# A two-layer attention and expert kernel: first tokens and first queries prepared one stage early, choices spread two pairs ahead, 64-row masks

## The reference

```python
xn = layernorm(x)
s = attention0(xn)            # 16 heads of 8, scores_content + scores_pos, softmax, @ Wo + bo
g = silu(expert_of_argmax(xn))  # 8 experts, one chosen per token, D x D each, with bias
x = x + s * g
xn = layernorm(x)
s = attention1(xn)            # 8 heads of two 8-wide halves, causal:
                              #   softmax(half 0) - lam * softmax(half 1), then rms norm, @ Wo
g = silu(top-2 of 8 experts)  # each 128 -> 256 -> 128 with gelu
x = x + s * g
```

## Time and profile before

| | us |
|---|---|
| median of 3 runs | 2071.6 (2067.59 to 2082.31) |
| profiled execution, its own time | 2077.91 |
| its span, first to last instruction | 2076.1 |
| token stage 0 | 0 to 213 |
| attention stage 0 | about 216 to 1203 |
| token stage 1 | about 1205 to 1519 |
| attention stage 1 | about 1522 to 2076 |
| PE busy over the span | 1767.2 (85%) |
| DVE, ACT, POOL busy | 1325.2 (64%), 1195.4 (58%), 1146.4 (55%) |

### The profile page before, as it was taken

One profiled execution on the slowest core, in us unless ns is written; L12 is line 12 of the kernel. 1 busy time (PEld: TensorE's weight loads), 2 busy tenths in 40 slices (PEclk: granted clock), 3 DMA queues, 4 the chain that ended last, 5 costly groups with the idle time before them and its releaser, 6 DMA issues. The chain is left out here.

```text
span 2076.1 us, 78586 instructions
## 1 busy us (share of the span) xinstructions
PE 1767.2 (85%) x34080; PEld 1327.7 (64%) x34080; DVE 1325.2 (64%) x1965; ACT 1195.4 (58%) x1438; POOL 1146.4 (55%) x1502
## 2 busy tenths in 40 slices
PE   5887489998898998989999759999968978879886
PEld 4666377777777776778877536666735545546554
DVE  5442367777676766877777424445467868867883
ACT  2322167777677766777877623344416645656555
POOL 4742469997699858998898621221112333333433
PEclk9887699999999999999999869999979989979998
DMA  3456312123221241222121121133220131121110
GB/s 104 129 146 191 93 52 66 48 65 96 73 65 59 67 106 60 68 68 59 55 62 55 52 91 53 57 95 88 80 61 18 30 66 26 41 52 30 26 26 16
DMA packets 166300, 139.97 MB, mean 67 GB/s; under 512 B 91715, under 2 KB 157014, under 8 KB 160454
## 3 DMA queue, kind: packets, MB, share of 16 engines
q1 hardware_dynamic: 153370, 105.93, 17.9%
q10 hardware_dynamic: 7212, 16.42, 3.3%
q0 software_dynamic: 5376, 12.59, 2.2%
HBM read 90.98 MB, written 43.12 MB: 65 GB/s over the span
## 5 line engine op out<-in xcount | busy, mean ns | idle before, releaser
L1306 ACT ACTIVATE a_EX<-bank 128x1024 f32<-128x1024 f32 x624 | 616.1, 1025 | 292.4 <-PE bank L1178 227.4
L1425 DVE TENSOR_TENSOR a_PM<-bank,a_PM 128x1024 f32<-128x1024 f32 x336 | 402.2, 1222 | 169.0 <-PE bank L1178 156.8
L1265 POOL TENSOR_TENSOR a_SN<-a_SN,a_MB 128x1024 f32<-128x1024 f32 x176 | 421.1, 2429 | 46.3 <-DMA a_MB<-m_dram 45.1
L1448 DVE TENSOR_REDUCE a_M<-bank 128x2 f32<-128x1024 f32 (+3 forms) x304 | 340.3, 1165 | 85.5 <-PE bank L1191 54.9
L1388 PE MATMUL bank<-a_EX,VV 128*32 128x128 f32 x9984 | 360.0, 288 | 3.5 <-issue 1.8
L1178 PE MATMUL bank<-QS,KS 51*128 51x128 bf16 (+1 forms) x4992 | 237.9, 230 | 89.5 <-DMA QS<-a_MP 38.1
L1388 PEld LDWEIGHTS bank<-a_EX,VV 128*32 128x32 f32 x9984 | 270.8, 115 | 52.1 <-issue 22.9
L1178 PEld LDWEIGHTS bank<-QS,KS 51*128 51x128 bf16 (+1 forms) x4992 | 160.1, 100 | 183.1 <-issue 57.6
L1302 ACT ACTIVATE a_SN<-bank 128x1024 f32<-128x1024 f32 x176 | 177.2, 1026 | 93.6 <-PE bank L1158 92.5
L1310 ACT ACTIVATE a_SN<-a_SN 128x1024 f32<-128x1024 f32 x176 | 185.4, 1058 | 38.8 <-POOL a_SN L1265 38.5
L1158 PE MATMUL bank<-QP,rel_t 112*128 112x32 bf16 x5632 | 197.7, 177 | 1.4 <-issue 1.2
(11 more groups left out here) (151 smaller groups left out, 2487.8 us busy)
## 6 DMA issues: line engine op xcount, KB each, us to landing
a_MB<-m_dram SPq DMA_DIRECT2D x32, 1024.0 KB, 4.9
QS<-q_dram SPq DMA_DIRECT2D x192, 96.0 KB, 3.0
KS<-k_dram ACTq DMA_DIRECT2D x12, 768.0 KB
q_dram<-t_PARTS SPq DMA_DIRECT2D x32, 192.0 KB, 2.8
k_dram<-t_PARTS SPq DMA_DIRECT2D x16, 384.0 KB, 2.9
QS<-a_MP SPq DMA_DIRECT2D x384, 2.0 KB
q_dram<-t_PARTS SPq DMA_DIRECT2D x32, 128.0 KB, 2.6
k_dram<-t_PARTS SPq DMA_DIRECT2D x16, 256.0 KB, 2.9
```

Source lines behind the costliest of these rows:

```text
L1265: pool.tensor_tensor(near_view(sn), near_view(sn), as_near(MB[:, :, :], it.part), ALU.add)\
L1306: act.activation(as_banks(EX[:, it.need % ER[layer]], part), by_head, ACT.Exp, scale=SCALE).then_inc(act_done, 1)
L1425: dve.tensor_tensor(pm, mb.rearrange("p hh (k i) -> p hh k i", k=4), pm, ALU.max).then_inc(max_used, 1)
L1448: dve.tensor_reduce(target.rearrange("p (hh k) -> p hh k", hh=2)[:, :, p0:p0 + g], mb[:, :, 0:g * width].rearrange("p hh (k j) -> p hh k j ...
```

## The change

- POOL permutes the queries of units 0 and 1 of layer 0 at the end of token stage 0 (after `parts` of the last group) instead of at the start of the attention stage; `permute` is now a helper.
- The first group of layer 1 (loading X, statistics, reciprocal root, normalisation) moves into attention stage 0: POOL loads X1 at `final` of unit 28, DVE takes the statistics after `final` of unit 30, POOL computes the root before its `final` of unit 31, DVE normalises before its `final` of unit 31. SP loads the q, k and v projections of layer 1 at `final` of unit 28. Their buffers lie in the half of KR that layer 0's batch 2 has left.
- SP no longer ends a token stage with the wait for `g_stored`; POOL waits for the group of the unit in `load_xg`, and ACT for all groups before it writes OS for unit 0 (OS and G now share memory). The exponentials for lam move to ACT's start of attention stage 0, after the key loads, and the rest to DVE's `final` of unit 0.
- The choice of pair 0 is spread at front 6, that of pair 1 at front 7, and at expert step k the choice of pair k+4 after the wait for HM of pair k.
- A mask tile is 4 matmuls of 256 columns: for each half of the queries (or keys) a weight table of 64 x 128 selects, and a moving table of 64 x 64, repeated for four heads, carries the values; the output has a step of two floats.
- For layer 1 the planner's mask cost goes from 480 to 260, and AIM, NEAR_BY and STAY are new. Layer 0's plan is the same.

```diff
-        "mask": 480, "evict": 1028, ...
+        "mask": 260, "evict": 1028, ...
-    {"max": (-0.94, 0.96), "mrow": (-5.54, -2.26), "msplit": (-1.51, -3.76), "exp": (1.3, 0.81),
-     "av": (4.27, -0.7), "out": (2.15, 1.46)}]
-NEAR_BY, STAY = (179, 222), (0.55, 1.3)
+    {"max": (-0.89, 0.93), "mrow": (-5, -1.11), "msplit": (-2.16, -1.22), "exp": (1.31, 0.71),
+     "av": (4.53, -0.91), "out": (2.07, 1.41)}]
+NEAR_BY, STAY = (179, 493), (0.55, 0.47)
...
+        OS = sb("OS", [P, 512])
+        G = OS[:, :].rearrange("p (t d) -> p t d", d=P)
+        spare = KR[:, 0, :, :].rearrange("p a s -> p (a s)").bitcast(F32)
+        X1 = spare[:, 0:512].rearrange("p (t d) -> p t d", d=P)
+        XN1 = spare[:, 512:1536].rearrange("p (c t d) -> p c t d", c=2, d=P)
...
+        def permute(pool, u):
+            r, q = u % NR, u % QR
+            pool.wait_ge(q_in[0][q], 64 * (u // QR + 1))
+            for a in range(2):
+                ... (the two copies and the drain, as before)
...  token stage, POOL
-                    scale(0)
-                    load_x(1)
-                    scale(1)
+                    if layer == 0:
+                        scale(pool, layer, 0)
+                    fetch_x(1)
+                    scale(pool, layer, 1)
...
                     parts(GROUPS - 1)
+                    if layer == 0:
+                        for u in range(NR):
+                            permute(pool, u)
...  token stage, SP
-                    sp.wait_ge(g_stored, 16 * GROUPS + 1)
...  token stage, ACT and DVE: the lam steps are taken out
-                        act.wait_ge(lam_sum, 1)
-                        act.activation(lam_s[:, 0:2], lam_s[:, 0:2], ACT.Exp).then_inc(lam_exp, 1)
...  token stage, PE
                             if k % 2 == 0:
-                                if k + 2 < E:
-                                    spread_choice(f, k + 2)
                                 pe.wait_ge(xm_ready, f * (E // 2) + k // 2 + 1)
+                                if k + 4 < E:
+                                    spread_choice(f, k + 4)
...
-                        if kind == "front" and k == 7 and layer == 0:
-                            spread_choice(f, 0)
+                        if kind == "front" and k >= 6 and layer == 0:
+                            spread_choice(f, 2 * (k - 6))
...  attention stage
-                for part in range(2):
+                for half in range(2):
                     for hh in range(2):
                         rows = slice(hh * HALF, (hh + 1) * HALF)
-                        last = pe.matmul(bank[:, 2 * it.n + hh, :].rearrange("p (h c) -> p h c", h=4), mask_b[rows, 0, part, :],
-                                         mask_b[rows, which, part, None, :].broadcast_to([HALF, 4, P]), start=False,
-                                         stop=part == 1, skip_group_check=True)
+                        out_h = bank[:, 2 * it.n + hh, :].rearrange("p (h c a) -> p h c a", h=4, a=2)[:, :, :, half]
+                        last = pe.matmul(out_h, mask_b[rows, which, half * P:(half + 1) * P],
+                                         mask_b[rows, which, None, 2 * P:].broadcast_to([HALF, 4, HALF]), start=False, stop=True,
+                                         skip_group_check=True)
...  SP, at final of a unit in layer 0
+                                if u == UNITS - 4:
+                                    sp.wait_ge(av_done, spare_free)
+                                    load_projections(sp, 1)
...  POOL
                     def load_xg(u):
+                        pool.wait_ge(g_stores[layer], 16 * (row_of(u) // GT + 1) + 1)
...
+                        if it.kind == "perm" and u >= NR:
+                            pool.wait_ge(act_psum, it.need + 1)
+                            permute(pool, u)
...
                         elif it.kind == "final":
+                            if layer == 0 and u == UNITS - 1:
+                                scale(pool, 1, 0)
...
+                            if layer == 0 and u == UNITS - 4:
+                                pool.wait_ge(av_done, spare_free)
+                                for r in range(2):
+                                    pool.wait_ge(stored[r], 16 * GT // 2)
+                                load_x(pool, 1, dst, X1, 0)
...  ACT
                     load_kv(layer, act, 1)
+                    if layer == 0:
+                        act.wait_ge(lam_sum, 1)
+                        act.activation(lam_s[:, 0:2], lam_s[:, 0:2], ACT.Exp).then_inc(lam_exp, 1)
...  DVE, at final
+                            if layer == 0 and u == UNITS - 1:
+                                normalise(dve, 1, X1, XN1, 0, 0)
                             dve.wait_ge(s_psum, u + 1)
...
+                            if layer == 0 and u == UNITS - 2:
+                                statistics(dve, 1, X1, 0)
```

More of the change, by code:

```diff
@@ L428, in build @@
         lam_exp = sem("lam_exp")
+        x_ins, x_frees, xn_readies, var_readies, rstd_readies, g_stores, proj_ins = (
+            [sem(f"t{layer}_{name}") for layer in range(2)]
+            for name in ("x_in", "x_free", "xn_ready", "var_ready", "rstd_ready", "g_stored", "proj_in"))
+        perm_done = sem("perm_done")
+        for k, name in enumerate("qkv"):
+            w[name, 1] = spare[:, 1536 + k * P:1536 + (k + 1) * P]
         lam_sum = sem("lam_sum")
@@ L1037, in body @@
                                .then_inc(g_ready, 1)
-                        if kind == "stats":
-                            statistics(f)
-                        if kind == "norm":
-                            normalise(f, p)
+                        if kind == "stats" and (f or layer == 0):
+                            statistics(dve, layer, X, f)
+                        if kind == "norm" and (f or layer == 0):
+                            normalise(dve, layer, X, XN, f, p)
                             if layer == 0 and f == 0:
@@ L1112, in attention_stage @@
             AV, MISC = 2 * SLOTS2, 2 * SLOTS2 + 1
+            far_end = max(n for n, it in enumerate(plan["pe"]) if it.kind in ("max", "exp") and it.u < UNITS - NB)
+            spare_free = min(it.k for it in plan["pe"][far_end:] if it.kind == "av") + 1
             def block_of(u):
@@ L1487, in _ @@
                             r = u % 2
+                            if layer == 0 and u == 0:
+                                dve.wait_ge(lam_exp, 1)
+                                dve.tensor_tensor(lam_s[:, 2:3], lam_s[:, 1:2], lam_s[:, 0:1], ALU.subtract)
+                                dve.drain()
+                                dve.tensor_scalar(lam_s[:, 3:4], lam_s[:, 2:3], -LAMBDA_INIT, None, ALU.add)
+                            if layer == 0 and u == UNITS - 1:
+                                normalise(dve, 1, X1, XN1, 0, 0)
                             dve.wait_ge(s_psum, u + 1)
@@ L1522 @@
         "eye": np.eye(P, dtype=np.float32),
-        "mask": np.tile(np.stack([np.eye(P), np.where(i[None, :] > i[:, None], -BIG, 0.0),
-                                  np.where(i[:, None] > i[None, :], -BIG, 0.0)]).reshape(3, 2, HALF, P).transpose(2, 0, 1, 3),
-                        (2, 1, 1, 1)).astype(np.float32),
+        "mask": causal_tables(i),
         "rank": np.broadcast_to((E - np.arange(E)).astype(np.float32), (P, GT, E)),
```

151 lines of the change are left out of this document (77 added, 74 removed).

## The result

The changed kernel takes 2058.3 us (median of 8 runs, 2048.9 to 2062.0) against 2081.0 for the kernel before (8 runs beside it, 2067.6 to 2085.9): ratio 0.9898, 95% interval 0.9876 to 0.9919, about 21 us of gain. Forecast were 48.7. The profiled executions took 2055.5 (span 2053.7) and 2077.9 (span 2076.1).

| | token stage 0 | attention stage 0 | token stage 1 | attention stage 1 |
|---|---|---|---|---|
| before | 216.1 | 988.7 | 317.3 | 554.0 |
| after | 211.0 | 977.8 | 307.4 | 557.5 |

The account below looks back on a forecast made before the run. It saw holes of about 20.7, 14.7 and 2.4 us at three block starts, and no single bound within attention stage 1. Terms 20 + 10.5 + 2.2 + 16 = 48.7 off 2071.6 gave 2023 us, range 1999 to 2051.

Parts of the forecast that it names:

- part 5: Masks in attention stage 1: half the columns save 30 us of TensorE, 17 if strided; stage 16 us shorter, bounds 0 to 30.
- part 6: New planner order in layer 1: no price in the trace, taken as 0, with 12 us either way.
- Part 1: Start of attention stage 0: hidden permutations and an earlier block end gain 20 us, Part 2 included; bounds 13 and 25.
- Rival (c): Attention stage 0: POOL's stall follows the permutations and holds unit 0 or 2; 8.5 us less gain, 2031 us; chance 0.05.
- Part 2: Token stage 0, choices two pairs ahead: TensorE's first-pair waits for HM go; 3.5 us, bounds 0 and 7.2.
- 8 x 0.90 = 7.2: Token stage 0: eight TensorE waits of 0.90 us for HM, at the groups' first pairs, all go.
- Part 3: Start of token stage 1: first transpose runs at block start, second group about 1 us late; 10.5 us, bounds 7.5 and 11.5.
- Part 4: Start of attention stage 1: the wait for the last gate store's landing goes; 2.2 us, bounds 1 and 2.4.
- 0.15 us for 256 at full clock instead of 0.107. Then 17 us would be left.: Masks' strided output, priced from the near tile's pieces of four: TensorE would still save 17 us.
- where TensorE is busy 93% of the time nearly all counts: Attention stage 1: mask saving shortens dense stretches almost fully, elsewhere DVE's maxima take over; 16 us from 27 on the chain.
- rival (d): Attention stage 1: masks give nothing and the order costs 12 us or more; 2054 us or a little above; chance 0.08.
- Rival (e): Attention stage 1: exponential tiles precede their maxima rows, TensorE waits every unit; slower, 2119 us at 3 us each; chance 0.04.

Follow-up runs that it names:

- e4: The changed kernel with SyncE issuing token stage 1's expert weights only after the second group of tokens has landed: 2054.2 us, ratio 0.9885 to the kernel before.
- e12: The earlier starts alone (masks and planner numbers of the kernel before), with token stage 1's expert weights behind the second group's landing: 2046.6 us, 0.9844.
- e16: The changed kernel with former planner numbers, masks written in runs of two floats with step four (landing on other tokens' scores): 2034.4 us, one execution.
- e6: The changed kernel with layer 1's former planner numbers and masks written side by side (landing on other tokens' scores): 2048.1 us, 0.9844.
- e17: The changed kernel with former planner numbers, masks written in runs of eight floats (landing on other tokens' scores): 2045.7 us, one execution.
- e18: e8 with one edit undone: POOL loads residual and gate rows in stored order, so layer 1's additions fall on other tokens: 2037.4 us, 0.983.
- e1: The changed kernel with each 256-column mask matmul written side by side instead of every second float (landing on other tokens' scores): 2058.1 us, 0.9903.
- e10: The changed kernel with layer 1's former planner numbers and DVE's row maxima reading only the first half of each key segment: 2030.4 us, 0.9762.
- e8: The changed kernel with token-order strided reads, correct side-by-side masks, gate and residual loads reordered, former planner numbers, expert weights behind second group: 2108.2 us, 1.0125.
- e7: The changed kernel with the masks and planner numbers of the kernel before, so the earlier starts alone: 2047.8 us, 0.9838.
- e2: The changed kernel with the old 512-column contiguous masks under the new planner numbers: 2059.6 us, 0.9913.
- e3: The changed kernel with layer 1's former planner numbers (mask cost 480, old aims, near-by and stay numbers), new masks kept: 2047.1 us, 0.9849.
- e13: e12 with the choices of token stage 0 spread one pair ahead, as in the kernel before: 2042.7 us, 0.9835.

## Why the prediction was wrong

The sum was 48.7; the runs give 33.4 for parts 1 to 4 (32.7 forecast), about 0 for part 5 (16 forecast) and about -12 for part 6 (0 forecast). So parts 5 and 6 failed, and inside the first four there are wrong steps that the total hides.

- **Part 1 was right in the hole it closed.** TensorE's first near tile follows the block's start by 0.2 us instead of 17.2, first maximum 219.32 (219.3 forecast), 20.3 us (20). From there to the last addition the stage took 966.3 us, 962.6 before. Rival (c), the stall that follows the permutations, did not come: 3.25 us, in unit 2, harmless. The block start of 211.0 (210.4 forecast) is in part luck: I had added it up from TensorE's last matmul, and that came at 204.78, not 209.1. The block waits for the landing of group 6's gate store instead, a term that the sum doesn't have. In the kernel before, that landing came at 212.1, half a microsecond ahead of TensorE's end, so the old trace names TensorE alone.
- **Part 2: the steps were wrong, the size about right.** The step "8 x 0.90 = 7.2" counts eight waits. They went, but six of them lie ahead of the wait for the v store, which takes most of their time back (it grew from 9.1 to 11.7 us, the wait one group earlier from 2.7 to 5.5), and the third pair's grew from 1.92 to 2.45. What remained came from where I had no term: a higher granted clock behind that wait, 7 us of TensorE, of which about 3 reach the block's end. The 3.5 us forecast lie near the 214.5 against 206.6 to 213.0 us of token stage 0, but by luck. One trace with one pair ahead stands against 17, and the whole time shows nothing of it (0.9844 with, 0.9835 without).
- **Part 3: 10.5 was too high by 3.** I gave the landing of the second group 3.7 us after the earlier trace rows. There it was the first group's load, issued 0.45 us behind the first of three small projection loads and 0.9 us ahead of the expert weights; behind the weights it took 7.7, and 3.2 and 3.5 with the weights held back (e4, e12). I had the doubled time as the lower bound, and it was the answer. The Trainium skill, "DMA: Bandwidth & Descriptors", section "SWDGE vs HWDGE vs iDMA", says that an engine goes round between the queues of POOL and of SP: by that rule, the trace agrees, and its 7.5 was nearer than my 10.5 (7.7 measured).
- **Part 4 was right**: the block's end follows the issue of the last gate store by 0.9 us instead of 2.8, and token stage 1 from its first expert matmul to the next stage's start took 284.9 us instead of 287.1 (2.2 forecast).
- **Part 5 failed twice.** The step that failed first: "0.15 us for 256 at full clock instead of 0.107. Then 17 us would be left." I took the near tile as nearest row for a strided output; its pieces are four floats long, and it writes at full pace like the runs of two in e16. The 0.59 us that I read holds the modelled end of its last matmul: from its start to that of the next line there are 0.40 us at 1.2 GHz for 8 x 64 columns, 0.10 for 256 at full clock, no price at all. A single float with a step of two costs 0.39 us a tile: 0.04 us of each tile's 0.43 are saved, where my 17 us needed 0.13. The Trainium skill, "PSUM — Partial Sum Buffer", section "Specifications (TRN2)", gives PSUM lines of 8 bytes and says that any non-contiguous pattern slows a matmul much; I had not weighed it. The runs agree for single floats, and contradict "any": two floats in a row, 8 bytes, already go at full pace.
- And the second: "where TensorE is busy 93% of the time nearly all counts". With the masks really short, 19 to 22 us less of TensorE shorten the stage by 3.6 us on average under the former order (e6, e16, e17, e18: 546.4, 545.8, 551.0 and 545.7, against 550.8) and by no more than the spread of the traces under the new one (e1: 559.2, against 557.5, 561.6 and 565.4). I had read the chain's 27 us of mask as time on the path; but a chain names what ended last, not how long before it the next one ended. In e6 DVE's maxima stand right behind, and in e10, with these halved, the maxima rows.
- **Part 6: 0 was the wrong middle.** Three pairs of kernels that differ in the order alone give 10, 12 and 16 us (0.9898 against 0.9849, 0.9903 against 0.9844, 0.9913 against 0.9838; each pair to some 8 us either way), their traces 7, 13 and 10 us, about my outer bound of 12. It is rival (d): masks nothing, order 12. I gave it 0.08 and left it out of the range. Rival (e)'s mechanism, exponential tiles ahead of their maxima rows, is what is seen, in weak form: 27 to 31 us of waits instead of 17. The prediction named both signs beforehand, masks above 60 us busy and over 20 us of waits for maxima rows; both came.

What stays open: why one set of planner numbers gives 17 us of those waits and every mixture 30 and more. Each set writes another order, and no single number carries it. Nor is it shown why the issue of the v store takes 21 us, why the granted clock is higher with two pairs ahead, and what makes POOL stand 18.4 us in e8; key loads were being issued at that time, as in the stall of the earlier trace rows.

## What to carry to other kernels

Price a strided output in PSUM from a row with the same run length; keep runs of two floats at least, or put a step of two on the bf16 moving operand, which showed no price here. When an engine gets work off it, look at what was due next behind each of its tiles: 22 us of TensorE bought 4 here, while three holes in which no engine worked gave back 33. Look for what was nearly as late as the thing you shorten: the gate store's landing, hidden behind TensorE before, ended the block after the change. An order written out by a planner is found as a set and has to be measured as one: here the starts and the old masks with the former order give 0.9838 (e7), with the new one 0.9913 (e2).

## What the runs showed of the hardware

- A mask matmul of 256 columns (bf16, 64 rows, in pairs) takes 417 ns in the trace (median) and 0.39 us per tile of four at full clock if each float is written two places from the next, 271 ns and 0.22 to 0.23 us if in runs of two, eight or 64 floats (e16, e17, e1). The 512 columns of the old masks take 0.43 us per tile. A bf16 moving operand with a step of two values: 229 ns on average for 128 columns, as without a step (e18, e3).
- A 256 KB load of POOL's queue lands after 7.7 us beside two megabytes of weights on SyncE's queue (the changed kernel) and after 3.2 and 3.5 us with those held back (e4, e12).
- POOL takes 0.86 and 0.80 us to issue a 64 KB load of 128 rows in de-interleaved order (e8), 0.59 and 0.54 us in stored order (e18), and once stood 18.4 us before such an issue, while ACT's key loads were under way.
- SyncE took 21.26 us to issue one v store right behind its key loads (20.40 before, 22.52 in e13); the same store took 0.61 us later in the stage.
- DVE's maximum takes 1.22 us over 1024 columns and 0.69 over 512 (e10), so halving them took 146 us off DVE, where I had expected 80, and 16 us off the stage. That kernel takes the maxima of half of the keys only, which bounds the exponentials less well; its 0.9762 is a measure of what the maxima cost, not a version to keep.
- The mean granted clock of TensorE over token stage 0 was 0.83 before and 0.85 in e13, with the choices one pair ahead, and 0.86 to 0.91 with two pairs. From the v-store wait to the last expert matmul it was 0.77 and 0.78 against 0.84 to 0.92, and the same matmuls took 44.7 and 44.3 us against 37.0 to 40.0. e12 (0.89) and e13 (0.78) differ in the order of issue alone.
